# PSUM operands and shared totals in a kernel's binning stage, and cell words read by fours in its count matrix stage

## What is computed

```python
x = _layernorm(x + _L0_gnn_ref(x, L0_gnn_W, L0_gnn_b, src, dst))       # mean over x[src] by dst
x = _layernorm(x + _L1_gnn_ref(x, edge_attr_128, edge_index_t, ...))    # edge messages both ways, mean
x = _layernorm(x + _L2_gnn_ref(x, edge_index, ...))                     # two attention layers, 4 heads
x = _layernorm(x + _L3_gnn_ref(x, src, dst, ...))                       # four mean layers, top-k between
```

## Time and profile before

| | |
|---|---|
| median of three executions | 8256.43 us |
| the profiled execution | 8261.7 us, span 8259.6 us |
| busy: PE, DVE, ACT, POOL | 6050.8, 4352.5, 2202.9, 3543.3 us |
| binning stage | from 0 to about 1277 us |
| count matrix stage | from about 1277 to about 2910 us |
| POOL scatters, line 365 | 832, 877.3 us busy, mean 1054 ns |
| POOL gathers, line 791 | 896, 903.6 us busy, mean 1008 ns |

### The profile page before, as it was taken

The page is one execution under the profiler, slowest core; times in us unless marked ns, Lnnn a source line. Parts: engine busy times, 40 slices in busy tenths (PEclk is TensorE's granted clock), DMA queues, the critical chain, the costliest instruction groups (busy, mean ns, idle before and its releaser), DMA issues. The chain is left out here.

```text
span 8259.6 us, 148729 instructions
## 1 busy us (share of the span) xinstructions
PE 6050.8 (73%) x38791; PEld 4220.4 (51%) x38792; DVE 4352.5 (53%) x11722; ACT 2202.9 (27%) x4944; POOL 3543.3 (43%) x3570
## 2 busy tenths in 40 slices
PE   0066643766666679999995777767777759996899
PEld 0055531444444345555555767757777735553455
DVE  9477755666766622222226777767777740103311
ACT  0022111433443310100004555535555510000200
POOL 4777776666666300000006777747777600000400
PEclk5578776888999989999998999979999979998999
DMA  0022212222222455677752222212222236664566
GB/s 18 17 70 70 70 44 66 90 93 88 96 97 88 74 157 172 182 181 187 184 147 63 55 54 54 55 47 54 55 55 55 52 111 190 189 198 116 142 194 179
DMA packets 835190, 849.31 MB, mean 103 GB/s; under 512 B 417948, under 2 KB 779131, under 8 KB 828348
## 3 DMA queue, kind: packets, MB, share of 16 engines
q1 hardware_dynamic: 710381, 560.82, 24.5%
q0 software_dynamic: 115904, 201.65, 10.6%
q10 hardware_dynamic: 8464, 81.36, 2.5%
HBM read 665.89 MB, written 97.31 MB: 92 GB/s over the span
## 5 line engine op out<-in xcount | busy, mean ns | idle before, releaser
L1937 POOL DMA_INDIRECT d_row_ring<-table_att,src_at x1664 | 1583.6, 952 | 641.0 <-issue 488.5
L2559 PE MATMUL psum<-e_a_ring,e_parts 128*128 128x448 bf16 x6174 | 1183.9, 353 | 76.1 <-DVE e_parts L2673 76.1
L791 POOL DMA_INDIRECT b_row_ring<-edge_attr,b_entry x896 | 903.6, 1008 | 590.2 <-SPq L768 350.1
L365 POOL DMA_INDIRECT listed<-a_record,a_slot_no x832 | 877.3, 1054 | 363.5 <-issue 271.6
L810 PE MATMUL psum<-b_hot 128*128 x2872 | 651.3, 366 | 401.9 <-DVE b_hot L995 265.8
L2559 PEld LDWEIGHTS psum<-e_a_ring,e_parts 128*128 128x128 bf16 x6174 | 604.9, 98 | 631.8 <-issue 80.0
L1346 PE MATMUL psum<-c_a_ring,c_parts 128*128 128x448 bf16 x4116 | 813.7, 356 | 43.9 <-DMA c_a_ring<-adjacency 39.3
L1962 PE MATMUL psum<-edges_out,edges_in 128*128 128x120 f32 x4896 | 702.2, 303 | 156.8 <-ACT edges_in L2028 155.8
L1962 PEld LDWEIGHTS psum<-edges_out,edges_in 128*128 128x128 f32 x4896 | 651.8, 214 | 203.0 <-issue 203.0
L995 DVE TENSOR_SCALAR b_hot<-b_iota,b_key_dst 128x896 int16 x1436 | 684.6, 477 | 2.4 <-issue 2.0
L1978 PE MATMUL psum<-edges_out,edges_in 128*128 128x132 f32 x4896 | 651.8, 288 | 16.9 <-DVE edges_out L2200 15.8
(11 more groups left out here) (472 smaller groups left out, 8296.1 us busy)
## 6 DMA issues: line engine op xcount, KB each, us to landing
e_a_ring<-adjacency SPq DMA_DIRECT2D x1029, 224.0 KB, 2.8
c_a_ring<-adjacency SPq DMA_DIRECT2D x686, 224.0 KB, 2.8
adjacency<-b_line ACTq DMA_DIRECT2D x49, 1568.0 KB
a_later<-edge_attr SPq DMA_DIRECT2D x103, 512.0 KB
d_row_ring<-table_att,src_at POOLq DMA_INDIRECT x1664
b_row_ring<-edge_attr,b_entry POOLq DMA_INDIRECT x896
listed<-a_record,a_slot_no POOLq DMA_INDIRECT x832
e_a_left<-adjacency_left SPq DMA_DIRECT2D x28, 224.0 KB, 3.3
```

What stands on the lines that cost most here:

```text
L365: pool.indirect_dma_start(out=listed, out_offset=bass.IndirectOffsetOnAxis(ap=slot_no[:, c:c + 1], axis=0), in_=record[:, c, :], in_offset ...
L791: pool.indirect_dma_start(out=row_ring[:, u % 4, g, 0:D], out_offset=None, in_=a["edge_attr_128"], in_offset=bass.IndirectOffsetOnAxis(ap= ...
L1937: pool.indirect_dma_start(out=row_ring[:, u % 4, g, :], out_offset=None, in_=table_att[layer], in_offset=bass.IndirectOffsetOnAxis(ap=src_ ...
L2559: mm = nc.tensor.matmul(psum[:, 2 * (turn % 2) + v, 0:WIN], (few_parts if d == 2 else parts)[:, piece, s, :], a_ring[:, (FIRST[turn] + s) ...
```

## The change

Binning: `placed` and the ones of the scan move from SBUF to PSUM (`ps_ones`, one element a partition, read again for each column); `ps_key` moves to the bank of `placed[2]`, so the key matmul is waited for and copied out ahead of the wide pass. The totals of odd tiles are taken by ScalarE, in place, with an accumulating activation; VectorE's pick for them has no count, and waits at the ring of four for ScalarE. The two record columns are copied by ScalarE instead of GpSimd, the bound on the count of the record comes behind the totals, and GpSimd's iota moves behind the transposes; its memset of ones goes.

Count matrix: a line has ROW = 8 words in `cell_row` instead of 7, the eighth with a count of zero, and the words are read as fours that start at multiples of four; CI grows from 3 to 4. All three engines read word row 1. The lines are split after window 3 instead of window 2. TURN becomes (2, 2, 2, 2, 2, 0), so pair codes too begin at multiples of four. On TensorE the cell words are loaded behind the first `two`. The loops over six lines carry a hint for their back edge.

```diff
-    CI = -(-CELLS // P)
+    ROW = 8
+    LAST = (NT - 1) * ROW + NWIDE - 1
+    CI = -(-NT * ROW // P)
     HOT = 4
+    PICKED = 3
     FIRST = P
     SEVEN = 7
-    TURN = (2, 2, 1, 2, 2, 1)
+    TURN = (2, 2, 2, 2, 2, 0)
...
-            ones_b = key_src[:, 0:TC].bitcast(BF16)
             is_tile = [sbb(f"is_tile{i}", [P, TC], I16) for i in range(4)]
-            placed = [sbb(f"placed{i}", [P, TC - FIRST]) for i in range(3)]
...
-            ps_key = [psum[:, k, 0:WIN] for k in range(2)]
+            ps_key = [psum[:, 4 + k, 0:WIN] for k in range(2)]
+            placed = [bank[k][:, 0:TC - FIRST] for k in range(3)]
+            ps_ones = bank[3][:, 1000:1001]
...
-                nc.gpsimd.memset(ones_b, 1.0)
...
-                nc.gpsimd.iota(iota[:], [[1, NP + P]], base=0, channel_multiplier=0)
...
-                pool.wait_ge(s_src_in, 48)
-                nc.gpsimd.tensor_copy(record[:, :, 2], ends[:, 0, :]).then_inc(s_record, 1)
                 nc.gpsimd.memset(record[:, :, 3], 0).then_inc(s_record, 1)
-                pool.wait_ge(s_dst_in, 48)
-                nc.gpsimd.tensor_copy(record[:, :, 1], ends[:, 1, :]).then_inc(s_record, 1)
                 pool.wait_ge(s_turned, 1)
+                nc.gpsimd.iota(iota[:], [[1, NP + P]], base=0, channel_multiplier=0)
                 nc.gpsimd.memset(edges_in[:], 0.0).then_inc(s_record, 1)
...
-                pe.wait_ge(s_totals, 1)
+                pe.wait_ge(s_totals, NT // 2 + 1)
...
-                pe.wait_ge(s_totals, 2)
+                pe.wait_ge(s_totals, NT // 2 + 2)
...
+                def turned():
+                    act.wait_ge(s_turned, 1)
+                    for at, k in ((src_at, 0), (dst_at, 1)):
+                        last = nc.scalar.copy(at[:].rearrange("p (u g) -> p u g", g=G),
+                                              bank[k].rearrange("p (g u) -> p u g", g=G)[:, 0:NB, :])
+                    last.then_inc(s_at, 1)
+                    nc.scalar.copy(dst_near.rearrange("p (u g) -> p u g", g=G),
+                                   bank[1].rearrange("p (g u) -> p u g", g=G)[:, 0:NB, :]).then_inc(s_at, 1)
+
...
-                act.wait_ge(s_turned, 1)
...
+                for b in range(1, NT, 2):
+                    if b == 9:
+                        turned()
+                        nc.scalar.copy(record[:, :, 2], ends[:, 0, :]).then_inc(s_record, 1)
+                    if b == 19:
+                        act.wait_ge(s_dst_in, 48)
+                        nc.scalar.copy(record[:, :, 1], ends[:, 1, :]).then_inc(s_record, 1)
+                    act.wait_ge(s_dve, PICKED + b)
+                    nc.scalar.activation(is_tile[b % 4][:], is_tile[b % 4][:], ACT.Identity, accum_out=totals[:, b:b + 1]).then_inc(s_totals, 1)
...
-                dve.wait_ge(s_const, 3)
-                V.tensor_scalar(record[:, :, 0], record[:, :, 0], E - 1, None, ALU.min).then_inc(s_record, 1)
                 dve.wait_ge(s_src_in, 48)
                 st.by(V.tensor_scalar(scratch[:], ends[:, 0, :], 7, None, ALU.logical_shift_right))
...
                 for b in range(NT):
                     st.settle(dve, picked[-4])
-                    picked.append(pick(b, slice(0, TC), totals))
+                    if b >= 5 and b % 2:
+                        dve.wait_ge(s_totals, b // 2 - 1)
+                    picked.append(pick(b, slice(0, TC), None if b % 2 else totals))
+                    assert st.k == PICKED + b
                 st.settle(dve)
                 dve.sem_inc(s_totals, 1)
+                dve.wait_ge(s_at, 2)
+                st.by(V.memset(ps_ones, 1.0))
+                dve.wait_ge(s_const, 3)
+                V.tensor_scalar(record[:, :, 0], record[:, :, 0], E - 1, None, ALU.min).then_inc(s_record, 1)
...
-                            mine = st.by(V.tensor_tensor_scan(placed[b % 3][:, 0:long], ones_b[:, 0:long], is_tile[b % 4][:, here],
+                            mine = st.by(V.tensor_tensor_scan(placed[b % 3][:, 0:long], ps_ones.broadcast_to([P, long]), is_tile[b % 4][:, here],
                                                               base[:, k, b:b + 1], ALU.mult, ALU.add))
...
-
-                dve.wait_ge(s_before, 2)
-                for k in range(2):
...
-                st.by(V.tensor_scalar(column_key, column_key, float(NWIDE), None, ALU.mult))
+                        dve.wait_ge(s_before, 2)
+                        for k in range(2):
+                            st.by(V.tensor_copy(column_key[:, k * WIN:(k + 1) * WIN], ps_key[k]))
...
+                        st.by(V.tensor_scalar(column_key, column_key, float(ROW), None, ALU.mult))
...
+            cell_real = sbb("cell_real", [P, CI], I32)
...
-            def befores(eng, q, n):
-                words = cell_row[0:1, 2, q:q + n] if isinstance(q, int) else cell_row[0:1, 2, bass.ds(q, n)]
-                return loaded(eng, words, 14)
...
-                def cells(s, first, end, before):
+                def cells(s, first, end, spans):
                     for w in range(first, end):
-                        at0, then = before[w - first:w - first + 2]
-                        n = nc.s_assert_within(pe.snap(then - at0), 1, COLS // 4,
-                                               skip_runtime_bounds_check_because="a cell has from four to all columns")
+                        _, n, at0 = spans[w % 4]
                         hold(pe, s_copied, s * (2 * NWIDE) + 2 * (last_use[w] + 1 + NWIDE), s_held_pe)
                         cell(ps_cell[buffer_of[w]], n, at0)
...
-                cells(0, 0, 3, befores(pe, 0, 4))
-                with pe.Fori(0, NT // len(TURN)) as i:
+                cells(0, 0, 4, spans_of(pe, 0, 4))
+                with nc.Fori(0, NT // len(TURN), engines=[nc.tensor.engine], hint_back_edge=True) as i:
                     for k, twos in enumerate(TURN):
                         s, m = i * len(TURN) + k, sum(TURN[:k])
-                        units = codes_of(pe, out_pairs, UNITS - 1, i * (2 * TURN_TWOS) + 2 * m, 2 * twos)
-                        before = befores(pe, i * (len(TURN) * NWIDE) + (k * NWIDE + 3), NWIDE + 1)
-                        two(i * TURN_TWOS + m, m % 2, units[0:2])
-                        cells(s, 3, NWIDE, before)
-                        if twos == 2:
-                            two(i * TURN_TWOS + (m + 1), (m + 1) % 2, units[2:4])
-                        cells(s + 1, 0, 3, before[NWIDE - 3:])
+                        if twos:
+                            units = codes_of(pe, out_pairs, UNITS - 1, i * (2 * TURN_TWOS) + 2 * m, 4)
+                            two(i * TURN_TWOS + m, 0, units[0:2])
+                        spans = spans_of(pe, i * (len(TURN) * ROW) + (k * ROW + 4), 8)
+                        cells(s, 4, NWIDE, spans[0:4])
+                        if twos:
+                            two(i * TURN_TWOS + (m + 1), 1, units[2:4])
+                        cells(s + 1, 0, 4, spans[4:])
                 two(TWOS - 1, 0, codes_of(pe, out_pairs, UNITS - 1, 2 * TWOS - 2, 2))
-                cells(NT - 1, 3, NWIDE, befores(pe, (NT - 1) * NWIDE + 3, NWIDE - 2))
+                cells(NT - 1, 4, NWIDE, spans_of(pe, (NT - 1) * ROW + 4, 4))
...
-                    for w, then in enumerate(befores(act, s * NWIDE + 1, NWIDE)):
-                        hold(act, s_hot_free, then * 2 + HOT, s_held_act)
+                    for w, (_, n, at0) in enumerate(spans_of(act, s * ROW, ROW)[0:NWIDE]):
+                        hold(act, s_hot_free, (at0 + n) * 2 + HOT, s_held_act)
...
+                st.settle(dve)
+                st.by(V.tensor_scalar(cell_real[:], cell_real[:], ROW - 1, None, ALU.bitwise_and))
+                st.settle(dve)
+                st.by(V.scalar_tensor_tensor(cell_i[:, 1, :], cell_real[:], float(NWIDE), cell_i[:, 1, :], ALU.is_lt, ALU.mult))
...
-                cells(0, 0, 3, spans_of(dve, 0, 3))
-                with dve.Fori(0, NT // len(TURN)) as i:
+                cells(0, 0, 4, spans_of(dve, 0, 4))
+                with nc.Fori(0, NT // len(TURN), engines=[nc.vector.engine], hint_back_edge=True) as i:
                     for k, twos in enumerate(TURN):
                         s, m = i * len(TURN) + k, sum(TURN[:k])
-                        pairs = codes(i * (2 * TURN_TWOS) + 2 * m, 4 + 2 * twos)
-                        spans = spans_of(dve, i * (len(TURN) * NWIDE) + (k * NWIDE + 3), NWIDE)
-                        cells(s, 3, NWIDE, spans)
-                        if twos == 2:
-                            turned_over(i * TURN_TWOS + m, m % 2, pairs[0:2], pairs[4:6])
-                            m, pairs = m + 1, pairs[2:]
-                        cells(s + 1, 0, 3, spans[NWIDE - 3:])
-                        turned_over(i * TURN_TWOS + m, m % 2, pairs[0:2], pairs[4:6])
-                cells(NT - 1, 3, NWIDE, spans_of(dve, (NT - 1) * NWIDE + 3, NWIDE - 3))
+                        if twos:
+                            pairs = codes(i * (2 * TURN_TWOS) + 2 * m, 8)
```

(15 more changed lines are left out.)

25 lines of the change are left out of this document (9 added, 16 removed).

## The result

The changed kernel takes 8151.44 us (median of four executions, 8145.02 to 8167.09), the kernel before, run beside it, 8257.06: a ratio of 0.9869, 95% interval 0.9855 to 0.9882, 1.3% faster. The profiled execution has a span of 8155.7 us against 8259.6.

What follows compares the result with a forecast made beforehand. GpSimd's row-by-row DMAs were taken to bound both stages. Start 18, plus pace 67, less 2 for the narrow pass and 9 for the count matrix stage, made 74 us: from the median 8256.4 to 8182, range 8150 to 8215.

Steps and rivals of the forecast that it cites:

- off the path: Count matrix loop: some 80 to 130 us of TensorE's holes go, without shortening the stage, which GpSimd's gathers and landings pace.
- The start: Binning, up to the first scatter: VectorE begins picks earlier and shares totals with ScalarE; gain 18 us (8 to 27).
- The pace: Binning, first 128 scatters: with PSUM operands they take 167 us instead of 233.8; gain 67 us, 52 at the lower end.
- the slack: Binning, wide pass: VectorE is done 145 us after the first scatter, before the scatters' 167; 22 us to spare.
- (c): Rival, binning: each VectorE op that touches PSUM pays a fixed sum more; 8207 us at 0.5 us a turn; chance 0.07.
- (d): Rival, binning: a scan writing PSUM runs slower and VectorE bounds the first 128 scatters; up to 8305 us shown; chance 0.05.
- the 2 us of the sum for the narrow pass: Binning, narrow ranking pass: PSUM operands cost VectorE 0.05 us a turn, 2.5 us on the path, 2 in the sum.
- The table: Count matrix stage, before its loop: CI of 4 instead of 3 adds products, reductions and longer rows; cost 6 us.
- The tail: Count matrix stage, behind the last unit: 21 cells instead of 18, 8 us less 5 for shorter loads; cost 3 us.
- The supply: Count matrix stage, chain of gathers, landings and slot frees: unchanged at 1443 us, perhaps shifted by 20 us either way.
- Back edge and loads: Count matrix loop, TensorE: the 3.55 us back edge might vanish, the 1.93 us loads fall to about 0.6; no shorter stage.
- The stage as a whole: Count matrix stage: 9 us slower, with a range from 15 us faster to 30 us slower.

Runs made afterwards that it cites:

- `ahead`: The changed kernel, but SP frees the next unit before it waits for the landing of the one before: 8023.09 us, ratio 0.9705.

## Why the prediction was right, and where not

**What bounds the kernel.** Right: both stages are paced by GpSimd's row DMAs, and what TensorE and VectorE gained in the cell words stayed off the path. `ahead` shows it by removing the chain.

**The start.** Right in sum and nearly in each term: VectorE at 10.07 (10), two held picks with a surplus of 9.0 us (9), ScalarE's pitch 0.88 (0.95), totals matmul at 52.63 (54), first scatter 97.21 (near 98).

**The pace.** Right: 62.6 for 67. In the wide pass a scatter comes every 1.33 us instead of 1.28, since the plain pick holds one of the two in each turn (1.09 against 0.97): 49 x 0.12 = 6 us, the kind of cost that the forecast had at its lower end, with 0.3 for each pick, and left out of its value. VectorE was done 143.6 us behind the first scatter (forecast 145): it waited 34.50 us for the all-reduce, 101.04 before, so the slack held. I took the step whole, though; the experiments part it into an operand that carries all of the gain and one whose hold, in this rhythm, costs next to nothing. The Trainium skill (SBUF — State Buffer, Who interferes with whom) lists the ops that take the port pair shared with GpSimd and says that one with two SBUF inputs contends with GpSimd's reads; the traces agree for the scan (2.35 us) and for the predicated copy (1.39). Its rule that a 2-port mode blocks the other for the whole instruction agrees where the pick waits for an iota (4.90 us) and where a scatter waits for the rest of a pick (1.09). The forecast set that second rule aside because of the earlier trace rows; the median gather there does not show what a scatter beside a pick pays.

**The rivals on VectorE.** (c) and (d) fell. The scan took 1.69 us with PSUM operands against 1.67, the copy 0.94 against 0.91, together the 0.05 us a turn that I took. But the turns did not grow by it: from scan to scan a wide turn went from 2.65 to 2.66 us, and 48 narrow turns took 38.41 us before (74.39 to 112.80) and 38.41 after (54.90 to 93.31). So the 2 us of the sum for the narrow pass did not come; the start alone, 72.11 to 52.63, is the whole 19.5. The 0.065 us for each op that I drew from the Trainium skill (VectorE: DVE Perf Modes, the errata cycle table) would be 0.13 a turn: more than measured.

**The table** was 4.8 for 6. **The tail** was mis-sized: 11.2 instead of 3. From TensorE's last wait for rows to the last full line's write it is 85.3 us (2703.18 to 2788.50) against 75.6: three more cells at 2.75 are 8.3, and the 5 us that I credited to shorter loads did not come.

**The supply** is the term that failed. The prediction said of the engines' savings that all of it is off the path, and gave the supply 20 us either way, for VectorE's is_src products. It moved by 30, 27 of them in a thing that I had not priced: the landing, which the chain holds 108 times, depends on what else is on the DMA queues at that moment, and the cell stage sets when its lines are written. How much of the 27 comes by these writes is open between the two ways of counting above. The trace of before showed it: 1408.9 us of SP's waits are eight gathers a unit and landings between 2.1 and 8.7 us, and I used only their mean. So the step failed in this, that the supply was taken as free of the engines' timing, when only its slots were. Back edge and loads did what they should (0.37 for 3.55 us, 0.59 for 1.93), with no effect of their own on the end that a run shows. The stage as a whole came out 13.7 us faster (4.8 - 29.7 + 11.2), where the sum had it 9 slower, near the end of its range of -15 to +30: that the time lies in the forecast's range, 1.4 us above its lower bound, is in part luck.

## What to carry to other kernels

Where a queue engine waits for each transfer before it frees the next slot, price the landing as a term of its own, and look first whether the free can go ahead of the wait: here that single reordering, on top of the change, was worth more (by the ratios 0.9705 against 0.9869, 1.6%) than both parts of the change together (1.3%). Beside GpSimd's DMAs, count the SBUF inputs of each VectorE op that runs at the same time, and look how much of the op is left when the DMA begins. Here one operand of a long scan in PSUM, a single broadcast element, freed the scatters, while the copy's hold cost next to nothing, because after its first turn the scatter met only its last 0.27 us. And in a stage bound by a chain, faster engines still move the moments of their own bulk writes, which can land on the chain or beside it.

## What the runs showed of the hardware

- An indirect DMA on GpSimd takes 0.97 us where nothing holds it. If it begins while a VectorE op has more than 0.2 us left, and the op is a scan of two SBUF operands, a predicated copy with mask and data in SBUF, or a plain compare, it ends 0.76 to 0.84 us behind that op (2.35, 1.39 and 1.09 us in the rows above). With the ones or the copy's data in PSUM it took 0.97.
- A plain compare of VectorE (0.37 us) that began beside a write-only iota or memset of GpSimd ended only 0.2 us behind it (4.90, 4.79 us); the counting form of the same compare did not (1.00 us).
- A load of eight registers from an aligned place costs 0.59 us on TensorE, 1.93 when it is not aligned; the hinted back edge costs 0.37 us instead of 3.55.
- Where a unit's last row gather ended within 4 us behind the issue of a 1568 KB write, the next free slot came 5.1 us behind the gather instead of 2.8; beside a write of an eighth of it, 3.0.
- For a time the same kernels took 10.8 ms, with holes of 75 to 87 us in the instruction flow of TensorE in the batch loop. No run settles why.
